# Causal masks in a two-layer attention decoder: added by VectorE in the score banks, in place of TensorE's mask products

## What is computed

```python
# layer 0: RMS norm, cross attention over the context, 16 heads of 64
q, k, v = rms(x) @ wq, ctx @ wk, ctx @ wv
x = x + softmax(q k^T) v @ wo
# layer 1, sub-block 1: causal self attention, 16 heads of 16
h = mha(ln1(x), ln1(x), causal=True)     # scores = where(tril, q k^T / 4, -inf)
x = x + h @ m_proj
# sub-block 2: cross attention over the context, 16 heads of 16
x = x + mha(ln2(x), ctx, causal=False) @ c_proj
# sub-block 3
x = x + relu(ln3(x) @ f_w1 + f_b1) @ f_w2 + f_b2
```

## Time and profile before

| | before |
|---|---|
| median of 3 runs | 5192.05 us (5190.23 to 5194.09) |
| the profiled execution's own time | 5187.58 us |
| its span, first to last instruction | 5185.8 us |
| busy: PE / weight load / ACT / DVE / POOL | 4998.9 / 4123.6 / 4157.3 / 3033.2 / 698.7 us |
| PE granted clock, mean | 0.990 |
| DMA | 337.76 MB, 65 GB/s over the span |

### The profile page before, as it was taken

How to read it: one execution, slowest core, us unless ns; L and a number is a source line. 1 busy time by engine, 2 the same in 40 slices (tenths; PEclk the granted TensorE clock), 3 DMA queues, 4 the chain that set the end, 5 groups by cost and what they waited for, 6 DMA issues and landing times. The chain is left out here.

```text
span 5185.8 us, 148766 instructions
## 1 busy us (share of the span) xinstructions
PE 4998.9 (96%) x49240; PEld 4123.6 (80%) x49240; DVE 3033.2 (58%) x7921; ACT 4157.3 (80%) x17044; POOL 698.7 (13%) x1227
## 2 busy tenths in 40 slices
PE   6999999999999999999999999999999999999996
PEld 5788888888888888888888888888888888888885
DVE  4555655665665666556556556656655665565563
ACT  4788888888888888888888888888888888888884
POOL 0111111111111111111111111111111111111110
PEclk8999999999999999999999999999999999999997
DMA  3112112112112121121121121121221211211211
GB/s 111 61 56 79 62 56 78 60 58 78 46 73 78 42 76 65 55 76 62 56 79 62 56 78 59 60 78 45 74 78 42 76 63 56 77 62 56 79 58 37
DMA packets 101414, 337.76 MB, mean 65 GB/s; under 512 B 8720, under 2 KB 66896, under 8 KB 68048
## 3 DMA queue, kind: packets, MB, share of 16 engines
q0 software_dynamic: 36576, 266.35, 13.9%
...
## 5 line engine op out<-in xcount | busy, mean ns | idle before, releaser
L606 ACT ACTIVATE ps<-ps,negmax 128x77 f32<-128x77 f32 (+2 forms) x6144 | 2063.4, 367 | 307.0 <-DVE negmax L823 305.3
L606 ACT ACTIVATION_READ_ACCUMULATOR ps<-ps,negmax 128x1 f32 x6144 | 1460.2, 244 | 0.8
L823 DVE TENSOR_REDUCE negmax<-ps 128x4 f32<-128x308 f32 (+2 forms) x1792 | 924.3, 563 | 222.1 <-PE ps L1094 90.6
L538 POOL TENSOR_TENSOR small<-small 128x1 f32<-128x1 f32 (+1 forms) x448 | 258.2, 576 | 2551.9 <-DVE small L800 2278.7
L995 PE MATMUL ps<-tail_h,coTh 128*128 128x256 f32 x2048 | 593.1, 290 | 3.4 <-DVE coTl L923 2.8
L818 DVE TENSOR_TENSOR zTl<-ps,zTh 128x256 fp32r<-128x256 f32 x512 | 210.6, 422 | 624.7 <-ACT zTh L586 624.5
L996 PE MATMUL ps<-tail_l,coTh 128*128 128x256 f32 x2048 | 572.0, 279 | 0.0
L997 PE MATMUL ps<-tail_h,coTl 128*128 128x256 f32 x2048 | 571.7, 279 | 0.0
L680 ACT ACTIVATE probs<-ps 128x512 f32<-128x512 f32 x768 | 399.6, 620 | 130.9 <-PE ps L1165 130.9
L995 PEld LDWEIGHTS ps<-tail_h,coTh 128*128 128x128 f32 x2048 | 385.3, 188 | 42.5 <-issue 34.9
L996 PEld LDWEIGHTS ps<-tail_l,coTh 128*128 128x128 f32 x2048 | 386.0, 188 | 0.0
...
## 6 DMA issues: line engine op xcount, KB each, us to landing
tail_h<-parted_f POOLq DMA_DIRECT2D x64, 1024.0 KB, 5.1
tail_l<-parted_f POOLq DMA_DIRECT2D x64, 1024.0 KB, 7.0
tail_h<-parted_wo POOLq DMA_DIRECT2D x63, 1024.0 KB, 5.2
tail_l<-parted_wo POOLq DMA_DIRECT2D x63, 1024.0 KB, 7.1
...
```

The source lines that it names most:

```text
L538: nc.gpsimd.tensor_tensor(rstd[:, stage, ts], veps[:, stage, ts], minus_half[:, ts], ALU.pow).then_inc(rstd_ready[stage], 1)
L606: ins = nc.scalar.activation(scores, scores, ACT.Exp, bias=negmax[w][:, t, h:h + 1], accum_out=sums[w][:, t, h:h + 1])
L823: nc.vector.tensor_reduce(dst, bank(s)[:, 0:heads * width].rearrange("p (h k) -> p h k", h=heads), AX_X, ALU.max, negate=True).then_inc(ma ...
```

## The change

The mask products L1113 and L1154 go, and with them the bfloat16 identity. Instead VectorE adds the mask in place in the PSUM bank, in a new function `mask`: one tensor_tensor add for each bank, over the diagonal blocks only, with the 128x128 bfloat16 `causal` (for `qsA`, `qsB`) or its transpose `causalT` (for `skA`, `skB`) broadcast over the heads. In `qsA` and `qsB` the maxima of a bank wait, on a VectorE semaphore (`chain`), for its add; in `skA` and `skB` ScalarE's exponential waits for `masked`, which the add raises, in place of PE's `full`. The three tables are written anew, with the adds as parts `m0` to `m3` of VectorE's order; `v0.0` and `qs0.1.3` are now done one turn earlier. The run of 30 satisfied waits on PE is 120 long. Of the tables the diff below shows two lines.

```diff
-RINGS = {"bank": 8, "split": 1, "chain": 1, "max": 1, "summed": 1}
+RINGS = {"bank": 8, "split": 1, "chain": 1, "max": 1, "masked": 1, "summed": 1}
...
-    "qsA": {"bank": 4, "max": 4}, "qsB": {"bank": 4, "max": 4}, "qs2": {"bank": 4, "max": 4},
-    "skA": {"bank": 4}, "skB": {"bank": 4}, "sk2": {"bank": 4},
+    "qsA": {"bank": 4, "max": 4, "chain": 4}, "qsB": {"bank": 4, "max": 4, "chain": 4}, "qs2": {"bank": 4, "max": 4},
+    "skA": {"bank": 4, "masked": 4}, "skB": {"bank": 4, "masked": 4}, "sk2": {"bank": 4},
...
-ctx+:2 qsB.0-:0347 v1-:1 norm.3.0 k0.0+:5 turn.3.0:6 stat.3.1 k0.1+:2 norm.3.1 turn.3.1:1 qsA-:5437 ln.1-
...
+stat.3.1 v1-:4 norm.3.1 qsA-:5302 turn.3.1:7 k0.1+:6 k0.0+:1 qsB.1-:4637 v0.0+:1 h.1:0 qs0.0.1+:2 h.3:5
...
-            nc.gpsimd.tensor_copy(identb[:], ident[:]).then_inc(consts_made, 1)
+            nc.gpsimd.affine_select(out=causalT[:], in_=causalT[:], compare_op=ALU.is_ge, fill=MASKED, base=0,
+                                    pattern=[[1, P]], channel_multiplier=-1).then_inc(consts_made, 1)
...
                     elif n in ("skA", "skB"):
-                        s = landed(u, r)
+                        (s, _, _), (_, _, total) = u["bank"][r], u["masked"][r]
+                        act.wait_ge(masked, total)
                         nc.scalar.activation(probs_slot(step, r), bank(s), ACT.Exp).then_inc(free[s], 1)
...
+            def mask(u, r, heads, tile, at, added):
+
+                s, v, _ = u["bank"][r]
+                dve.wait_ge(full[s], v)
+                scores = bank(s).rearrange("p (h k) -> p h k", h=heads)[:, :, at:at + P]
+                nc.vector.tensor_tensor(scores, scores, tile[:].unsqueeze(1).to_broadcast([P, heads, P]),
+                                        ALU.add).then_inc(added, 1)
+
             def maxima(u, j, dst, heads, width):
                 s, v, _ = u["bank"][j]
+                if "chain" in u and "summed" not in u:
+                    dve.wait_ge(chain, u["chain"][j][1])
...
+                    elif n in ("skA", "skB"):
+                        mask(u, int(r[1:]), 2 if n == "skA" else 4, causalT, 0, masked)
...
+                        if str(r).startswith("m"):
+                            mask(u, int(r[1:]), 4, causal, 0, chain)
...
+                            mask(u, int(r[1:]), 2, causal, P, chain)
...
-            for _ in range(30):
+            for _ in range(120):
                 pe.wait_ge(consts_in, 16 * 4)
...
-                        for s, _, _ in u["bank"]:
-                            heads = 4 if n == "qsA" else 2
-                            diagonal = bank(s).rearrange("p (h k) -> p h k", h=heads)[:, :, 512 // heads - P:]
-                            pe.matmul(diagonal, identb[:], causal[:].unsqueeze(1).to_broadcast([P, heads, P]),
-                                      start=False, stop=True, skip_group_check=True).then_inc(full[s], 1)
+                                if n == "qsB" or m == KT - 1:
+                                    ins.then_inc(full[s], 1)
...
-                        for r in range(4):
-                            s = take_bank(u, r)
-                            diagonal = bank(s).rearrange("p (h q) -> p h q", q=cols)[:, :, 0:P]
-                            pe.matmul(diagonal, causal[:], identb[:].unsqueeze(1).to_broadcast([P, len(heads), P]),
-                                      start=True, stop=False, skip_group_check=True)
```

More of the change, by code:

```diff
@@ L43 @@
 LOOP_ORDER_TEXT = """
[L44 to L48, removed]
@@ L49 @@
-ctx+:2 qsB.0-:0347 v1-:1 norm.3.0 k0.0+:5 turn.3.0:6 stat.3.1 k0.1+:2 norm.3.1 turn.3.1:1 qsA-:5437 ln.1-
-h.0:6 h.1:2 q0.3+:0 qs0.0.1+:1 qs0.1.1+:3 h.3:2 h.2:4 mt.1-:6 tr0.0.1+:5 skA.0-:7601 qs0.0.0+:5 skB-:2734
-f2.0:0 qs0.1.0+:4 qs0.0.3+:6 pv.1.0-:5 skA.1-:7231 f2.1:0
+pv.1.1:2 tr0.0.0-:6 qs0.0.2-:5 rms+ norm.0+ proj.1.0:1 proj.1.1:6 tr0.1.1-:4 stat.2.0 tr0.1.0-:3 stat.2.1
+qs0.1.2-:2 pv0.1-:1 pv0.0-:7 norm.2.0 norm.2.1 v0.1-:6 turn.2.0:1 turn.2.1:4 tr0.1.2-:0 turn.0+:3 tr0.0.2-:7
+q1.2:6 tr0.0.3-:2 tr0.1.3-:1 qs2.1:6735 pv0.2-:0 pv0.3-:1 qs2.0:2640 q0.2+:1 wo.0-:3 stat.1.0- norm.1.0- ln.2
@@ L52 @@
+q0.3+:7 wo.1-:3 stat.1.1- mt.2:2 norm.1.1- turn.1.0-:4 sk2.0:1706 sk2.1:5432 ck-:1 pv.2.0:6 turn.1.1-:0
+pv.2.1:7 k1-:4 proj.2.0:6 stat.3.0 proj.2.1:0 q1.1-:3 norm.3.0 cv-:2 ctx+:4 qsB.0-:7061 turn.3.0:2 q0.1+:3
+stat.3.1 v1-:4 norm.3.1 qsA-:5302 turn.3.1:7 k0.1+:6 k0.0+:1 qsB.1-:4637 v0.0+:1 h.1:0 qs0.0.1+:2 h.3:5
+q0.0+:4 h.0:7 ln.1- mt.1-:4 qs0.0.0+:6 tr0.0.1+:0 skA.0-:3451 qs0.0.3+:7 h.2:0 skB-:1254 qs0.1.1+:6 f2.0:3
+qs0.1.0+:1 qs0.1.3+:4 pv.1.0-:3 skA.1-:7620 f2.1:5
 """
 ACT_ORDER_TEXT = """
-pv.1.1 v0.0 tr0.1.1 tr0.0.0 qs0.1.3 qs0.0.2 v0.1 pv0.1 tr0.1.0 turn.2.0 turn.2.1 tr0.1.3 qs0.1.2 pv0.0 q1.2
@@ L58 @@
[L58 to L62, removed]
+pv.1.1 tr0.0.0 qs0.0.2 tr0.1.1 tr0.1.0 pv0.1 qs0.1.2 pv0.0 v0.1 turn.2.0 turn.2.1 tr0.1.2 turn.0 tr0.0.2 q1.2
@@ new lines @@
+tr0.0.3 tr0.1.3 qs2.1/0 pv0.2 pv0.3 qs2.1/3 qs2.1/2 qs2.1/1 qs2.0/0 qs2.0/1 qs2.0/3 qs2.0/2 ln.2 q0.2 q0.3
+mt.2 turn.1.0 sk2.0/3 sk2.0/0 sk2.0/1 sk2.0/2 sk2.1/3 sk2.1/1 sk2.1/2 sk2.1/0 turn.1.1 pv.2.0 ck pv.2.1 k1
+q1.1 cv ctx turn.3.0 qsB.0/1 q0.1 qsB.0/0 qsB.0/2 v1 qsB.0/3 turn.3.1 qsA/1 k0.1 qsA/3 k0.0 qsA/2 qsA/0
+qsB.1/0 qsB.1/1 qsB.1/3 qsB.1/2 ln.1 qs0.0.1 q0.0 v0.0 mt.1 tr0.0.1 qs0.0.0 skA.0/2 skA.0/1 skA.0/3 skA.0/0
+qs0.0.3 skB/0 qs0.1.1 skB/3 skB/1 skB/2 qs0.1.0 qs0.1.3 pv.1.0 skA.1/3 skA.1/0 skA.1/2 skA.1/1
@@ L63 @@
 """
 DVE_ORDER_TEXT = """
[L65 to L69, removed]
@@ L70 @@
[L70 to L71 removed]
+rms pv.1.1 qs0.0.2/0 norm.0 proj.1.0 proj.1.1 stat.2.0 stat.2.1 qs0.1.2/0 norm.2.0 pv0.1 qs0.0.2/1 norm.2.1
+qs0.1.2/1 pv0.0 turn.2.1 turn.2.0 turn.0 qs2.1/0 qs2.1/3 qs2.1/2 qs2.1/1 pv0.2 pv0.3 qs2.0/0 qs2.0/1 qs2.0/3
+qs2.0/2 wo.0 stat.1.0 norm.1.0 ln.2 wo.1 stat.1.1 turn.1.0 norm.1.1 turn.1.1 pv.2.0 pv.2.1 proj.2.0 stat.3.0
+proj.2.1 norm.3.0 stat.3.1 ctx qsB.0/m1 qsB.0/1 qsB.0/m0 qsB.0/0 qsB.0/m2 turn.3.0 qsB.0/2 norm.3.1 qsB.0/m3
@@ L72 @@
+qsB.0/3 qsA/m1 qsA/1 qsA/m3 turn.3.1 qsA/3 qsA/m2 qsA/m0 qsA/2 qsA/0 qsB.1/m0 qsB.1/0 qsB.1/m3 qsB.1/m1
+qsB.1/m2 qsB.1/3 qsB.1/1 qsB.1/2 h.1/0 qs0.0.1/0 h.1/1 h.3/0 h.3/1 ln.1 qs0.0.1/1 h.0/0 qs0.0.0/0 h.0/1
+skA.0/m2 skA.0/m1 skA.0/m3 qs0.0.0/1 skA.0/m0 qs0.0.3/0 h.2/0 h.2/1 skB/m0 qs0.1.1/0 qs0.0.3/1 skB/m3 skB/m1
+skB/m2 qs0.1.1/1 f2.0 qs0.1.0/0 qs0.1.3/0 qs0.1.0/1 qs0.1.3/1 skA.1/m3 skA.1/m0 skA.1/m2 skA.1/m1 pv.1.0 f2.1
 """
```

29 lines of the change are left out of this document (15 added, 14 removed).

## The result

The changed kernel takes 5219.7 us (median of 5 runs, 5212.85 to 5221.54), the kernel before, beside it, 5191.9 us (5187.95 to 5194.09): ratio 1.0051, 95% interval 1.0037 to 1.0066. It is slower by 0.5%, where the forecast was 5024 us. 5219.7 lies outside the range, on the side that had a chance of 9 in 100.

A forecast was written before the change was run, and what follows sets the result against it. PE's order of work was taken as the bound: 3.48 us a batch removed less 0.85 given back in waits, times 64, is 168 us off 5187.6, 5019; the runs' median 4.5 us higher gives 5024 us, range 4945 to 5130.

The forecast's parts named there:

- What bounds the kernel now: PE's order of work: 77.4 us of a 78.72 us turn; whatever leaves it shortens the turn by its slot.
- the layout further down: New order laid out step by step from qsB.0 with measured distances; waits of PE sum to 4.6 us a turn.
- What is removed: Mask products on PE in qsA, qsB, skA, skB: slots of 3.48 us a batch, 223 us over 64 batches.
- What is added: 24 in-place PSUM adds a batch on DVE, 0.42 or 0.69 us each: 12.2 us, DVE busy 78%.
- What is moved, and what is late next: New order's hand-overs to PE: waits of 4.6 us a turn, so 0.85 of 3.48 us given back.
- the subtraction: PE's new waits of 4.6 us a turn less at most 3.8 now: 0.8 to 0.9 us given back.
- The 90 further waits: Satisfied waits on PE ahead of the loop, hidden in the wait for the first batch: 0, bounds 0 and 47 us.
- The rivals: Waits unchanged or fewer, 4970 to 4930 us (0.28); up 1.5 to 3 us, 5065 to 5160 (0.15); slower (0.09); PE's clock falls.
- slower: ACT chain behind the adds, qsB.0 to skA.0, becomes the bound from 3.48 us of new waits: 5290 or 5410 us; 0.09.
- The clock: PE's granted clock in the steady part stays at 1.00; a fall got 1 in 100, counted under slower.
- the signs of being wrong: Adds well above 0.42 us, clock below 1.00, PE busy under 93%, or ACT's waits on adds several times today's on maxima.
- the three waits foretold: Signs of being right: v0 waits on ACT's copy of k0bd, pv.1 on DVE's f2.0 result, mt.1 on the q0 copy.

The follow-up runs named there:

- e5: Changed kernel's code with the tables of before, causal mask left out altogether, 150 satisfied waits ahead of PE's loop: 5070.11 us, ratio 0.9771.
- e13: The kernel before with its 30 satisfied waits made 120, nothing else: 5192.07 us, ratio 1.0006.
- e7: The changed kernel with 30 satisfied waits in place of 120: 5590.03 us, ratio 1.0775.
- e1: The changed kernel with the adds and their waits taken out, so no causal mask is computed: 5147.27 us, ratio 0.9916.
- e4: The changed kernel's tables with the mask products back on PE and no adds on VectorE: 5288.62 us, ratio 1.0191.
- e15: The changed kernel with v0.0 put back behind pv.1.1 on PE and ScalarE, adds kept: 5354.27 us, ratio 1.0317.
- e16: Changed tables with all mask products on PE, no adds, and v0.0 back behind pv.1.1: 5324.69 us, ratio 1.0263.
- e6: Changed kernel's code with the tables of before, VectorE's adds put in by hand, 150 satisfied waits: 5664.98 us, ratio 1.0927.

## Why the prediction was wrong, point by point

**What bounds the kernel now.** "Whatever leaves PE's order shortens the turn by its slot, as long as the two others keep up" is the first step that failed. PE had 1.0 us of waits a turn, and the time at which ACT and DVE would have been ready was only just hidden: with no mask at all and the old order, the turn falls by 1.75 us of 3.48 (e5). For the kernel before, "keep up" was tested only by sums of busy time (ACT 85%, DVE 78%), and a chain has no such sum; the layout further down tested places, but of the new order alone. It has to be tested at each hand-over: how long before PE asks is the result there? At `h.0` the answer was less than 1.1 us.

**What is removed.** The slots were right where nothing waits behind them: 0.37, 0.55 to 0.58 and 0.86 us freed (e5), against 0.37, 0.54 and 0.95. `qsA`'s 0.71 and `qsB.0`'s 0.37 freed nothing, since `h.0` waits behind both. An estimate by the 131 ns that the Trainium skill gives for a product over 512 columns (TensorE: Matmul & The Clock Gate, "Back-to-back issue gap") is 0.52 us freed at `skB`; e5's turns show 0.86, and the measurement decides.

**What is added.** The prices are right: 0.423 and 0.690 us. DVE is busy for 72% in the steady windows, not 78%: its busy time, counted once where records overlap, rose by (3660.3 - 3033.2) / 64 = 9.8 us a batch and not 12.2, and the turn is longer.

**What is moved, and what is late next.** The layout was good, place by place: `v0.0` was to start 12.2 us behind `qsB.0` and did so at 12.21, with a wait of 1.03 us (0.9 forecast; the terms given for PE's way there add up to 11.24 us and not 11.5, and with the right sum the forecast wait is 1.05); `mt.1` waits 0.59 (0.75), `qs2.0` 0.59 (0.75), `pv.2.1` 0.5 (0.3), `sk2.0` 0.3 (0.25), `pv.1.0` 0.26 (0.8). `pv.1.1`'s 0.5 us I had not seen; `skB` and `f2.0` have none. The sum is 3.9 us a turn, 4.6 forecast. **The step that failed is the subtraction: "against at most 3.8 now. So 0.8 to 0.9 us of the 3.48 is given back".** The 4.6 were idle times of PE; the 3.8 were 1.0 us of idle PE and 2.8 us of late weight loads, which the prediction itself had called mostly hidden. Like taken from like, 4.6 - 1.0 = 3.6 us of new waits use up the 3.48: a turn of 78.84 us, 8 us above before, at the edge of no change. That is worked out afterwards, but from the forecast's own numbers. The runs bear this out. All idle time of PE is 4.7 us a turn after and 1.4 before (the windows above), 3.3 us more. In the forecast's mixed currency, PE's and the weight loads' waits on ACT and DVE together, 50.0 + 143.9 us became 194.3 + 405.7 in 1000 to 5000 us, from 3.8 to 11.9 us a turn, while the turn grew by 0.46: such a sum prices nothing. The rest, up to the 3.94 us that were given back in all (3.48 + 0.46), is 0.6 us by which PE's own work shrank less than by its slots, 77.4 to 74.5 us a turn. Slots next to waits are longer: 2024.89 - 2023.64 = 1.25 us from `qsB.0` to what follows it, 2010.01 - 2008.86 = 1.15 before. Why isn't shown.

**The 90 further waits.** "30 of them left no trace there ... I take 0" failed. I looked for their own time, and that is nothing (e13: 1.0006). They move the loop's code, and with 30 waits the changed kernel would have taken 5590 us (e7). The bounds of 0 and 47 us didn't hold what the edit does.

**The rivals.** The clock stayed at 1.00, as forecast. The side that came true, "slower", had the right point of decision, 3.48 us of new waits a turn, but named a single chain between `qsB.0` and `skA.0` and twice the price of adds. Neither was needed: seven hand-overs of 0.3 to 1.0 us did it, five of them without any add (e1), and four of these with the mask products still in place (e4). ACT's waits on adds (113.5 us over the span) stand where its waits on scores stood before (130.9), so their total shows no cost; what the adds delay shows ahead of `pv.1.1`, 24.5 us in 1000 to 5000 us. Of the signs of being wrong, only PE's share over the span (92%) came; adds, clock, ACT's waits and the three waits foretold were as they should be for 5024 us. None of the signs put a bound on PE's idle time a turn, which is where the forecast failed.

**What stays open.** Why the new order by itself costs 98 us: its five waits are shown (e4) and that `v0.0`'s move isn't the cause (e15, e16), but which of the other moves makes them wasn't found. Nor was the best place of the adds in the old order sought; e6's 595 us hold for one order written by hand.
